# Row maxima taken in key halves five tiles of a head ahead and carried to their row by a DMA, two projection banks, four key places, in a two-layer attention kernel

## The reference

```
h   = group_norm(x)                                   # 32 groups
q, k, v = qkv_w @ h + qkv_b                           # 8 heads of 64 channels
a   = softmax(q^T k / sqrt(64), over the keys)        # 1024 x 1024 for each head
x1  = x + proj_w @ (a v) + proj_b
```

## Time and profile before

| | us |
|---|---|
| median of 3 runs | 3624.24 |
| the profiled execution | 3620.22 |
| its span, first to last instruction | 3618.5 |
| TensorE busy in the span | 3021.4 |
| VectorE busy | 2099.5 |
| ScalarE busy | 1656.3 |
| mean granted TensorE clock | 0.941 |

### The profile page before, as it was taken

One profiled execution on the slowest core, in us unless ns is written; L12 is line 12 of the kernel. 1 busy time (PEld: TensorE's weight loads), 2 busy tenths in 40 slices (PEclk: granted clock), 3 DMA queues, 4 the chain that ended last, 5 costly groups with the idle time before them and its releaser, 6 DMA issues. The chain is left out here.

```text
span 3618.5 us, 34889 instructions
## 1 busy us (share of the span) xinstructions
PE 3021.4 (83%) x12880; PEld 2329.7 (64%) x12880; DVE 2099.5 (58%) x2585; ACT 1656.3 (46%) x1999; POOL 431.9 (12%) x193
## 2 busy tenths in 40 slices
PE   3898998899899988988998998899873777787777
PEld 2566676667667666766776676667653665566565
DVE  4567657666765675676567656665633534444452
ACT  2456546554554565465455645554532221222211
POOL 1002101201200120011002101101010111110001
PEclk9899999999999999999999999999996888888888
DMA  5212122223212221311222132223102111111100
GB/s 202 62 36 59 44 85 62 67 56 96 59 36 79 71 62 47 105 53 53 65 76 62 42 93 59 62 58 94 36 33 84 42 40 36 45 46 41 41 35 23
DMA packets 112649, 221.26 MB, mean 61 GB/s; under 512 B 31616, under 2 KB 31872, under 8 KB 112000
## 3 DMA queue, kind: packets, MB, share of 16 engines
q1 hardware_dynamic: 112512, 219.42, 19.8%
HBM read 143.34 MB, written 42.21 MB: 51 GB/s over the span
## 5 line engine op out<-in xcount | busy, mean ns | idle before, releaser
L452 ACT ACTIVATE p_high<-ring 128x1024 fp32r<-128x1024 f32 x512 | 525.5, 1026 | 758.9 <-PE ring L369 758.9
L556 DVE TENSOR_REDUCE row_max<-pmax 128x1 f32<-128x1024 f32 x512 | 623.7, 1218 | 374.0 <-PE pmax L343 373.0
L563 DVE TENSOR_TENSOR p_low<-p_full,p_high 128x1024 fp32r<-128x1024 f32 x512 | 739.7, 1445 | 15.3 <-ACT p_full L455 13.6
L455 ACT ACTIVATE p_full<-ring 128x1024 f32<-128x1024 f32 x512 | 522.2, 1020 | 0.0
L343 PE MATMUL pmax<-k_high_low,q_high_high 128*128 128x512 f32 x1024 | 348.9, 423 | 86.6 <-DVE row_max L556 86.6
L385 PE MATMUL pv<-p_high,v_high 128*128 128x512 f32 x1024 | 413.6, 404 | 1.3 <-ACT num_den L463 1.3
L386 PE MATMUL pv<-p_high,v_low 128*128 128x512 f32 x1024 | 404.6, 395 | 0.0
L300 PE MATMUL fill<-h_high,w_high 128*128 128x512 f32 x768 | 316.8, 412 | 103.0 <-DVE k_high_low L574 60.2
L392 PE MATMUL pv<-p_low,v_high 128*128 128x512 f32 x1024 | 336.1, 410 | 50.6 <-DVE p_low L563 50.6
L719 POOL TENSOR_TENSOR o_normed<-num_den,o_normed 64x1024 f32<-64x1024 f32 x64 | 182.3, 2848 | 1580.9 <-DMA o_normed<-rec_rows 1579.2
L369 PE MATMUL ring<-q_low_max,k_high_one 65*128 65x512 f32 x1024 | 329.9, 404 | 0.7 <-ACT q_low_max L445 0.7
(11 more groups left out here) (164 smaller groups left out, 3898.8 us busy)
## 6 DMA issues: line engine op xcount, KB each, us to landing
x_tiles<-in_x SPq DMA_DIRECT2D x64, 512.0 KB, 4.0
w_high<-w_split SPq DMA_DIRECT2D x128, 256.0 KB, 2.7
w_low<-w_split SPq DMA_DIRECT2D x128, 256.0 KB, 3.0
k_high_one<-k_high_low SPq DMA_DIRECT2D x128, 128.0 KB, 2.3
q_high_high<-q_high_high SPq DMA_DIRECT2D x128, 128.0 KB, 2.3
o_normed<-rec_rows SPq DMA_DIRECT2D x64, 256.0 KB, 3.5
x<-x_tiles SPq DMA_DIRECT2D x32, 512.0 KB, 5.1
x_full<-x SPq DMA_DIRECT2D x32, 512.0 KB, 3.3
```

Of the source, the lines that this page charges most:

```text
L452: nc.scalar.activation(ph[:, r, :], ring[:, r, :], ACT.Exp, scale=ATT_SCALE).then_inc(s_ph, 1)
L455: nc.scalar.activation(p32[:, r, :], ring[:, r, :], ACT.Exp, scale=ATT_SCALE).then_inc(s_p32, 1)
L556: nc.vector.reduce_max(mcol[:, h % 2, i:i + 1], pmax[:, :], AX_X).then_inc(s_mx, 1)
L563: tt(pl[:, r, :], p32[:, r, :], ph[:, r, :].bitcast(F32), ALU.subtract).then_inc(s_pl, 1)
```

## The change

Seven edits, all in layer 0.

1. **Row maxima in key halves.** `pmax` is one bank instead of two. A tile is taken as two halves of 512 keys: one matmul, one reduction over 512, twice. The first half stands at the start of a step, the second behind the score matmuls of the same step. `row_max` gets a column for each half, and every four tiles VectorE takes the larger of the two (`top_of_halves`, 128x4).
2. **Half a head ahead.** Each step of every head takes one tile: steps 0 to 2 tiles 5 to 7 of the head itself, steps 3 to 7 tiles 0 to 4 of the next head (`AHEAD = 3`).
3. **Their row by DMA.** The eight transposes and ScalarE's negation are gone. A tile takes every fourth query (`first:first + HALF - 3:4`), so four columns of a partition are four neighbours in the row, and one DMA of 128 runs of 16 bytes writes half a row of `q_low_max`. The row of ones in `k_high_one` is -1. The scores wait for it at steps 0 and 4.
4. **Two projection banks.** `fill2` has two banks used in turn, so a unit waits for the readout of the unit before the last.
5. **Key places.** k has four places, q three; ScalarE's wait for a free place now stands at q.
6. **Order of the units.** k first, then q, then v; k and q halves lie two steps apart, a whole unit in one step (the tuple of parts is always both). In the first and third pair of a batch: k a0 and a2, q a4 and b0, v b1 and b2, `vt` b2 and b4. Second pair: the last three `o` units at a0 to a2, k a3 and a5, q a7 and b0, v b2 and b4, `vt` b5 and b7. Fourth: k a2 and a4, q a6 and b0, then as the second. The first five `o` units stay at b3 to b7 of the first pair.
7. **Side work.** Two places for weights instead of three. Statistics of the next batch at steps 1 to 4 of head 4 (before: heads 3 and 4), `group_scale` in head 5, POOL's normalisation ahead of `h_low` in head 5; before, it came behind.

```diff
+def max_tile(h, s):
+
+    if s < AHEAD:
+        return h, NT - AHEAD + s
+    return (h + 1, s - AHEAD) if h + 1 < ALL_HEADS else None
...
+        first = {0: 0, 1: 3, 2: 0, 3: 2}[kind]
+        if kind == 1:
+            spread(a, 3, ("k", n, 0))
+            spread(a, 5, ("k", n, 1))
+            put(a, 7, ("q", n, 0))
+        else:
+            spread(a, first, ("k", n, 0))
+            spread(a, first + 2, ("k", n, 1))
+            spread(a, first + 4, ("q", n, 0))
...
-W_SLOTS = 3
+W_SLOTS = 2
...
-                w = UNIT_ORDER[n - 1]
+                w = UNIT_ORDER[n - 2]
...
-                if i > 0:
-                    pe.wait_ge(s_mx, h * NT + i)
-                elif h > 0:
-                    pe.wait_ge(s_mrow, h)
-                s = slot_of(h)
-                for n in range(2):
-                    last = mm(pmax[:, n * HALF:(n + 1) * HALF], q1[:, s, i * P:(i + 1) * P],
-                              k1[:, s, n * HALF:(n + 1) * HALF], start=True, stop=True)
-                last.then_inc(s_max, 1)
-
-            def max_rows(h):
-                pe.wait_ge(s_mx, (h + 1) * NT)
-                for i in range(NT):
-                    last = nc.tensor.transpose(pmax[0:1, i * P:(i + 1) * P], mcol[:, h % 2, i:i + 1], ident[:, :])
-                last.then_inc(s_rows, 1)
+                m = (h * NT + i) * 2 + n
+                if m > 0:
+                    pe.wait_ge(s_mx, m)
+                first = (i // 4) * HALF + i % 4
+                mm(pmax[:, :], q1[:, q_slot(h), first:first + HALF - 3:4], k1[:, k_slot(h), n * HALF:(n + 1) * HALF],
+                   start=True, stop=True).then_inc(s_max, 1)
...
-                if s == 0:
-                    pe.wait_ge(s_mrow, h + 1)
+                if s % 4 == 0:
+                    pe.wait_ge(s_mrow[s // 4], 16 * (h + 1))
...
+                block = max_tile(h, s)
+                if block:
+                    take_max(*block, 0)
                 if t > 1:
                     weigh_low(t - 2)
...
                 scores(h, s)
...
+                if block:
+                    take_max(*block, 1)
+                for u, parts in PARTS.get((h, s), []):
+                    unit_work(u, parts)
+                if t > 0:
                     weigh_high(t - 1)
...
+                block = max_tile(h, s)
+                if block:
+                    reduce_max(*block, 0)
                 if t > 0:
                     p_low(t - 1)
...
+                if block:
+                    reduce_max(*block, 1)
+                    if block[1] % 4 == 3:
+                        top_of_halves(block[0], block[1] // 4)
                 for u in UNITS.get((h, s), []):
                     unit_low(u)
...
+            def max_to_row(h, i):
+                sp.wait_ge(s_mtop, 2 * h + i + 1)
+                row = q2[HD:HD + 1, q_slot(h), i * HALF:(i + 1) * HALF].bitcast(F32)
+                sp.dma_start(row.rearrange("o (p k) -> o p k", p=P), mtop[:, h % 2, 4 * i:4 * i + 4].bitcast(F32)
+                             ).then_inc(s_mrow[i], 16)
```

More of the change, by code:

```diff
@@ L130, in units_by_step @@
-        if g % PAIRS == 2 and g // PAIRS + 1 < BATCH:
-            put(a, 2, ("g", g // PAIRS + 1, 0))
-            put(a, 5, ("g", g // PAIRS + 1, 1))
-    return at
-UNITS = units_by_step()
+        a, b, n, b0 = 2 * g, 2 * g + 1, g + 1, g // PAIRS
+        kind = g % PAIRS
+        if kind == 0 and g > 0:
+            o = [("o", b0 - 1, t, i) for t in range(CT) for i in range(2)]
+            for s in range(5):
+                put(b, 3 + s, o[s])
+            for s in range(3):
+                put(a + 2, s, o[5 + s])
@@ L137 @@
+        if kind == 2 and b0 + 1 < BATCH:
+            put(a, 6, ("g", b0 + 1, 0))
+            put(b, 0, ("g", b0 + 1, 1))
+    return at
+PARTS = parts_by_step()
+UNITS = {at: [u for u, parts in us if 1 in parts] for at, us in PARTS.items()}
 UNIT_ORDER = PROLOGUE + [u for h in range(ALL_HEADS) for s in range(STEPS) for u in UNITS.get((h, s), [])] + EPILOGUE
-UNIT_STEP = {u: at for at, us in UNITS.items() for u in us}
 def piece_of(u):
@@ L302, in project @@
                     last = mm(fill[:, :], w2, high[:, c, cols], start=False, stop=(c == CT - 1))
-                last.then_inc(s_unit, 1)
+                if 1 in parts:
+                    last.then_inc(s_unit, 1)
             def turn_v(u):
+                fill = fill_of(u)
                 fill_free(u)
@@ L419, in _ @@
                 unit_work(u)
-            pe.wait_ge(s_dset, 5)
-            for i in range(NT):
-                take_max(0, i)
+            pe.wait_ge(s_dset, 4)
+            for i in range(NT - AHEAD):
+                for n in range(2):
+                    take_max(0, i, n)
             for h in range(ALL_HEADS):
@@ L693, in _ @@
                 unit_low(u)
-            for i in range(NT):
-                reduce_max(0, i)
+            for i in range(NT - AHEAD):
+                for n in range(2):
+                    reduce_max(0, i, n)
+            top_of_halves(0, 0)
             for i in range(4):
@@ L839, in step @@
                         twins(u)
+                if block and block[1] % 4 == 3:
+                    max_to_row(block[0], block[1] // 4)
                 if h > 0:
@@ L881, in _ @@
                     twins(u)
+            max_to_row(0, 0)
             for t in range(CT):
```

221 lines of the change are left out of this document (108 added, 113 removed).

## The result

| | before | after |
|---|---|---|
| median of 4 runs | 3623.65 (3618.6 to 3624.52) | 3698.31 (3691.16 to 3703.17) |
| span of the profiled execution | 3618.5 | 3695.5 |
| mean granted TensorE clock | 0.941 | 0.927 |

The ratio is 1.0201, with a 95% interval of 1.0174 to 1.0229: 2.0% slower. I had forecast 3599 in a range of 3558 to 3665. Sign and range are both wrong.

What follows compares the result with a forecast made beforehand. TensorE, busy 3021 of 3618 us, was taken to bound the kernel. Steps +4, start-up -20 and end -8 gave -24 from 3620.2, so 3596; the median lies 4 above, 3600, stated as 3599, range 3558 to 3665.

Steps and rivals of the forecast that it cites:

- Sum 308.3: Layer 0: the eight heads of a batch, added up from their steps, take 308.3 us before VectorE's side work.
- 327.2 against 325.2: Layer 0, middle batches: 327.2 us each with side work, against 325.2 before; +12 over six batches.
- The nearest rows say no change: Strided weight loads of the maxima's matmuls: forecast to cost nothing extra, judged by loads without a stride.
- `vt` step: Step that turns a v half: 3.2 us; its follower 4.3, or 3.8 with v half 1 in the same step.
- Start-up and end: Before scores begin: -20 us, bounds -10 to -27; the last eight `o` units at the end: -8 us.
- Wrong if: Signs against the forecast: L383 loads over 0.19 us, L404 waiting, or batches' steps more than 10 us from 327.
- Behind a k or q half: Next step's first reduction waits on VectorE behind the half: that step takes 4.8 us, 6.95 with a unit.
- rival 1: Strided weight loads of the maxima's matmuls are slower: up to +61 us, 3660 in all; chance 0.22.
- Side work: VectorE's added work per batch: 4.4 us for POOL's normalisation, 5.5 for statistics, 9 for head 5.
- The row of maxima: DMA of half a row per four tiles: lands before the scores need it, cost 0, bounds 0 to +26 us.
- Rival 2: VectorE's chain is tighter than drawn: at 0.2 us in some 30 of 64 steps, +48, 3647; chance 0.13.
- Rival 3: Waits hide better, with half reductions at 0.61 us and side work in unit steps: 3518 to 3575; chance 0.15.

Runs made afterwards that it cites:

- the run on the kernel before: Kernel before with the maxima's tiles taking every fourth query, the row's order left as it was: 3630.46 us, ratio 1.0019.
- neighbouring queries: Changed kernel with the maxima's tiles taken from 128 neighbouring queries instead of every fourth one, the row's DMA as it was: 3664.48 us, ratio 1.0115.
- turning: Changed kernel with v half 0 turned ahead of v half 1, not a step later, in each batch's second and fourth pair: 3659.65 us, ratio 1.0098.
- low parts later: Changed kernel with VectorE writing the low parts of k and q halves one step later, behind that step's reductions: 3546.87 us, ratio 0.9797.
- two banks of maxima: Changed kernel with two PSUM banks for maxima, one for projections, and v half 0 turned ahead of v half 1: 3632.27 us, ratio 1.0013.
- side work: Changed kernel with statistics moved to steps with a unit in heads 3 and 4, `normed_full` one step later in head 5: 3718.79 us, ratio 1.0244.
- both reorderings: Changed kernel with k and q low parts one step later and v half 0 turned ahead of v half 1: 3514.58 us, ratio 0.9692.
- all four: Changed kernel with k/q low parts later, v half 0 turned earlier, statistics and `normed_full` moved, neighbouring-query tiles with four row DMAs: 3563.41 us, ratio 0.9819.
- row first: Kernel of both reorderings with neighbouring-query tiles and four DMAs per half row, put ahead of SP's k or q copies: 3497.33 us, ratio 0.9641.
- statistics: Kernel of row first with only the statistics moved, to step 4 of head 3 and steps 0, 2, 4 of head 4: 3463.14 us, ratio 0.955.

## Why the prediction was wrong

**The step that failed** is the sum of the steps: "Sum 308.3" with its side work, "327.2 against 325.2", where a batch takes 340.0. Three of its terms were wrong: the strided load, put at nothing ("The nearest rows say no change"); the `vt` step, timed without ScalarE's one `v_full`; and TensorE's clock, taken over from the kernel before without a word. The steps were forecast at +4 and measured +111.5: 18 of the difference in the first batch, 77 in the next six, 13 in the last. Start-up and end came out at -27.7 and -6.8, against -20 and -8. Two of the signs named under "Wrong if" came true: loads longer than 0.19, and steps of a batch more than 10 us from 327.

Some of the prediction's sums are off as well. Its heads add up to 309.0 (the second pair's even head to 42.6, its odd one to 36.5, the first pair's odd one to 46.7), 0.7 a batch more; 240 + 45 is 10 less than 295, not 8; and 6 x 5.2 is 31, not 28. None of this changes the sign.

**Behind a k or q half**, 4.8 forecast: 4.95 (5.0 to 5.1 with a reciprocal in it, 5.5 and 5.2 in head 2, where the clock falls), 7.11 with a unit (6.95 forecast). The mechanism and the size were right, and the run with the low parts a step later shows that it is worth 151 us. It was in my sum, and set off against the better odd heads; so it doesn't explain the error of the forecast, but without it the change would have won. I had called it "the change's price"; at that it was priced rightly.

**The strided load** was rival 1, at 0.22, and it happened: 309 ns for 193, and 34 us by the run without it, some of them by way of the clock. I had bounded it at +61, flowing steps included; by the run on the kernel before, there is nothing or nearly nothing in these. "The nearest rows say no change" was a choice by rows that have no stride. The Trainium skill (SBUF — State Buffer, "Door 1: The DMA port swizzle", on cachelines) said what the sign would be: the trace agrees that a column a line apart makes the load longer, by 60%, and the run on the kernel before shows besides that it is nearly hidden where a matmul runs meanwhile (1024 such loads, +7 us).

**The `vt` step of pairs 2 and 4**, 3.2 forecast: 4.83, and its follower 4.62 for 4.3. I followed the units on TensorE and VectorE and not on ScalarE, whose `v_full` has one place. The prediction has no such term. By these steps it is 2 x 1.95 = 3.9 us a batch over the forecast; the run says 38 us in all, 4.8 a batch.

**Side work**, 9 for head 5 and 5.5 for the statistics: moving the statistics alone, once the low parts are out of the way, gives 34 us, about 5 a batch, so 5.5 was about the right size for them. Head 5 takes 47.1 in the row above, with 44.6 forecast. Its `normed_full` one step later made it 2.2 shorter and head 6 as much longer, and its three `p_low` beside POOL's work take 2.6, 4.3 and 2.9 in the mean, 6.2 us over 1.22 in sum, where I had added 3; no run takes it apart further. POOL's normalisation was priced by a `p_low` of 2.27; after, one beside it takes 3.01:

```profile
877.50 2.39 POOL L758 TENSOR_TENSOR o_normed<-num_den,o_normed 64x1024 f32<-64x1024 f32 x1 [50.33 <-DMA o_normed<-rec_rows]
...
877.96 3.01 DVE L600 TENSOR_TENSOR p_low<-p_full,p_high 128x1024 fp32r<-128x1024 f32 x1
```

But that is no new cost: the mean `p_low` is 1429 ns after and 1445 before, 13 and 14 us a batch over 1.22, so `p_low` beside POOL is as slow in the kernel before.

**The clock** is what I left out. Worked out from the traces' clock records, the time that TensorE spends at 1.2 GHz in the steps of the six middle batches, in us:

| before | changed | neighbouring queries | turning | low parts later | two banks of maxima |
|---|---|---|---|---|---|
| 65 | 160 | 137 | 150 | 92 | 174 |

| side work | both reorderings | all four | row first | statistics |
|---|---|---|---|---|
| 195 | 96 | 188 | 123 | 92 |

The changed kernel has 95 us more of it, 16 a batch. Matmuls are 0.43 us apart there for 0.23, so about half of it, 8 us a batch, is the most that it can cost; where TensorE waits anyway, it costs nothing. That is an estimate from one profiled execution of each kernel. The runs that lost more than I could explain (side work, all four) have the most of it.

Of the 12.8 us a batch by which I missed, the load is 34 / 8 = 4.3 and `v_full` about 4, both with what they do to the clock; 0.7 is my adding. That leaves some 4. The clock can fill it, and so can head 5; no run separates them, and it stays open. The first batch, 18 us over, is not taken apart either: its granted clock is 0.94 for 0.97.

**The row of maxima** is hidden, as forecast: landing 1.9 us in the median, 0.3 us of waits. In the run with all four edits it came late for the reason that the prediction weighed, SP's wait for a half ahead of it, once the low parts came a step later and the row took four DMAs.

**Rival 2** (a tighter chain on VectorE) doesn't hold: VectorE waits 6.3 us for `p_full` in the whole kernel, and with neighbouring queries the steps drawn at 3.0 and 4.8 take 3.03 and 4.85. **Rival 3** was right about one thing, that there was time to be had in the waits, and wrong that this change takes it: for that it gave 3518 to 3575.

## What to carry to other kernels

Cost a wait by what stands behind it in the queue: here the halved reduction needed 0.69 us of VectorE, and TensorE paid 1.8 at a step behind a k or q half for it, because an instruction that was still waiting for ScalarE stood in front of it. Before an instruction with a late input, ask whether anything behind it is already due; moving it one step later was worth more (151 us) than a second bank for the buffer it held up (31, net of what the bank taken from the projections cost). And follow every engine that a moved unit touches, with its single buffers, before adding up steps. If an edit adds waits to an engine whose clock falls and rises in the trace, don't carry the clock of before into the sum.

## What the runs showed of the hardware

- A weight load of 128 x 128 float32 whose columns are 16 bytes apart takes 309 to 314 ns, for 193 to 195 with neighbouring columns. Steps with a wait in them are 0.10 us longer by it, and 1024 such loads cost 7 us (4 to 10) in the kernel before, where most have a matmul to lie under.
- A `p_low` of 1.22 us takes up to 3.4 us beside POOL's normalisation or `o_low`, in both kernels, and up to 5.1 in the changed one beside its `h_low` (2.5 before).
- Four DMAs of 128 runs of 4 bytes take 2.54 us of SP's queue, one of 128 runs of 16 bytes takes 0.51; they land in about the same time (2.0 and 1.9 us in the median).
- The granted clock of head 0 of the third batch was 0.96 with waits of up to 1.2 us in its steps, and 1.00 in the kernel before with waits of up to 0.4. Behind waits of 1.45 and 0.20 TensorE ran at 1.2 GHz, with matmuls 0.43 us apart for 0.23. Where the clock falls, a wait is paid a second time; but head 3, with waits of up to 1.3 us, kept 1.00, and no run shows which waits bring the fall.
